# A second block with plain fc1 products, interleaved with block 0's fc2, and weight sums from a second load

## What is computed

```python
h = gelu(einsum('bnd,hd->bnh', x, fc1_w) + fc1_b)            # HID = 1024
shared = einsum('bnh,sh->bns', h, fc2_w) + fc2_b             # 192 outputs
expert = einsum('bnh,bph->bnp', h, experts_w[indices]) + experts_b[indices][:, None]  # 64 outputs
out = x + concatenate([shared, expert], axis=-1)
```

## Time and profile before

| | us |
|---|---|
| median of 3 runs | 380.73 |
| lowest and highest | 380.22, 380.85 |
| the profiled execution, its own time | 380.61 |
| its span in the profile | 378.8 |
| PE busy | 361.0 (95%) |
| ACT, POOL, DVE busy | 248.5, 232.8, 211.8 |

### The profile page before, as it was taken

One profiled execution on the slowest core, in us unless ns is written; L12 is line 12 of the kernel. 1 busy time (PEld: TensorE's weight loads), 2 busy tenths in 40 slices (PEclk: granted clock), 3 DMA queues, 4 the chain that ended last, 5 costly groups with the idle time before them and its releaser, 6 DMA issues.

```text
span 378.8 us, 7987 instructions
## 1 busy us (share of the span) xinstructions
PE 361.0 (95%) x2915; PEld 355.7 (94%) x2915; DVE 211.8 (56%) x357; ACT 248.5 (66%) x420; POOL 232.8 (61%) x105
## 2 busy tenths in 40 slices
PE   6952999999999999999999999999999999999996
PEld 5842999999999999999999999999999999999996
DVE  1477447567473747667373756757384756733331
ACT  2674357687675767777575768767576777755560
POOL 0780537766666777666667776666667766666490
PEclk9995799999999999999999999999999999999999
DMA  8769860616152250616244151626235032303011
GB/s 197 166 140 257 251 135 32 163 40 173 57 146 85 82 130 26 173 54 157 76 110 122 44 154 35 173 58 158 73 91 127 24 115 50 119 2 111 2 56 57
DMA packets 70433, 39.98 MB, mean 106 GB/s; under 512 B 39418, under 2 KB 70394, under 8 KB 70394
## 3 DMA queue, kind: packets, MB, share of 16 engines
q1 hardware_dynamic: 69776, 38.95, 39.0%
q10 hardware_dynamic: 618, 0.53, 0.7%
HBM read 27.92 MB, written 8.39 MB: 96 GB/s over the span
## 4 chain that ended last, share of the span: by engine, by line
PE 86%; issue 2%; POOL 1%; ACT 0%; DVE 0%; POOLq 0%
PE fc_ps L875 39%; PE acc_ps L911 16%; PE acc_ps L915 16%; PE acc_ps L913 16%; POOL ht L303 1%; ACT ht L460 0%; ACT gelu L483 0%; DVE work L710 0%; DVE resid L728 0%; POOLq L293 0%
## 5 line engine op out<-in xcount | busy, mean ns | idle before, releaser
L303 POOL TENSOR_TENSOR ht<-gelu,ht 128x1024 fp32r<-128x1024 f32 x64 | 154.8, 2419 | 115.2 <-ACT ht L460 115.2
L875 PE MATMUL fc_ps<-xt,w1t 128*128 128x256 f32 x1260 | 186.7, 284 | 3.8 <-DVE xt L678 3.8
L875 PEld LDWEIGHTS fc_ps<-xt,w1t 128*128 128x128 f32 x1260 | 167.5, 193 | 4.2 <-DVE xt L678 4.2
L911 PE MATMUL acc_ps<-w2t,ht 128*128 128x256 f32 x512 | 145.5, 284 | 0.1
L913 PE MATMUL acc_ps<-w2t,ht 128*128 128x256 f32 x512 | 145.4, 284 | 0.0
L915 PE MATMUL acc_ps<-w2t,ht 128*128 128x256 f32 x512 | 145.4, 284 | 0.0
L911 PEld LDWEIGHTS acc_ps<-w2t,ht 128*128 128x128 f32 x512 | 98.9, 193 | 0.3 <-POOL ht L303 0.3
L915 PEld LDWEIGHTS acc_ps<-w2t,ht 128*128 128x128 f32 x512 | 98.8, 193 | 0.0
L913 PEld LDWEIGHTS acc_ps<-w2t,ht 128*128 128x128 f32 x512 | 98.8, 193 | 0.0
L446 ACT ACTIVATE work<-fc_ps 128x512 f32<-128x512 f32 x30 | 17.9, 597 | 87.7 <-PE fc_ps L875 87.7
L460 ACT ACTIVATE ht<-gelu 128x1024 fp32r<-128x1024 f32 x64 | 67.8, 1059 | 3.5
(11 more groups left out here) (49 smaller groups left out, 236.5 us busy)
## 6 DMA issues: line engine op xcount, KB each, us to landing
resid<-in_x SPq DMA_DIRECT2D x16, 512.0 KB, 4.0
pieces<-in_L_cond_experts_w SPq DMA_DIRECT2D x128, 64.0 KB, 2.0
out<-resid SPq DMA_DIRECT2D x32, 256.0 KB, 3.2
pieces<-in_x SPq DMA_DIRECT2D x60, 128.0 KB, 3.6
w2t<-w2t SPq DMA_DIRECT2D x4, 768.0 KB, 8.0
bias<-in_L_cond_experts_b SPq DMA_DIRECT2D x32, 32.0 KB, 2.8
pieces<-in_L_cond_fc_w SPq DMA_DIRECT2D x4, 192.0 KB, 7.8
work<-in_L_cond_fc_w ACTq DMA_DIRECT2D x4, 128.0 KB, 5.8
```

What stands on the lines that cost most here:

```text
L303: nc.gpsimd.tensor_tensor(ht[:, slot, LO, :, :].rearrange("p k t -> p (k t)"), gelu[:, q % 2, :, :].rearrange("p k t -> p (k t)"), ht[:, s ...
L875: last = nc.tensor.matmul(fc1_ps[:, dst, j * SEQ:(j + 1) * SEQ], w1t[:, w, wv, ms], xt[:, n % 2, o, xv, :], start=(fresh and j == 0 and at ...
L911: nc.tensor.matmul(dst, h_hi_t, w_hi, start=(r == 0 and u % (2 * T) == 0), stop=True, skip_group_check=True)
```

## The change

Block 1 is now multiplied plainly too (`PLAIN = 2`), so the seven-product loop covers blocks 2 to 15, with all its counts of semaphores moved by one block.

- **PE.** The transposes of the weight sums (`s_bank`) are gone. After block 0's eight chunks come eight pairs of steps: four units of block 0's fc2, then one chunk of block 1's fc1. The chunks of block 1 are taken in the order of pairs 1, 3, 0, 2. fc2 of block 0 no longer waits for the weight sums, and waits for the second copy of fc2_w (`w2_row`) only at its fifth unit.
- **Weight sums.** After the fourth fc1_w transpose group SP loads fc1_w again over its first copy, in 32-row pieces (four DMAs of 256 KB, 256-byte rows). POOL waits for it, makes the four sums, and DVE transposes them (`s_square`) in the transpose bank; ACT and DVE split them as before, in the order 0, 2, 1, 3.
- **POOL.** The sums stand after pair_lo(0) and pair_lo(1) and before pair_lo(2) and pair_lo(3). The low parts of block 1's four pairs are made on DVE instead (`plain_low`).
- **x of block 1** is split whole by ACT and DVE (`x1_high`, `x1_low`).
- **DVE, ACT.** The first work is reordered: two fc2_w transposes ahead of the second half of fc1_w, the fc2_w transposes now in the accumulator banks; experts of block 1, the last `plain_low` and the first drain end DVE's prologue, ahead of the loop.
- **ACT's queue** loads the index first instead of last.

The core of the diff; the shifts of semaphore counts are left out.

```diff
+    PLAIN = 2
...
+    PAIR_ORDER = (1, 3, 0, 2)
...
+        def wait_h_lo(engine, q):
+            if q < PAIRS:
+                engine.wait_ge(h_lo, q + 1)
+            elif q < 2 * PAIRS:
+                engine.wait_ge(plain_lo, q - PAIRS + 1)
+            else:
+                engine.wait_ge(h_lo, q - PAIRS + 1)
+        def chunk_of(q, j):
+            r = q % PAIRS
+            return 2 * (PAIR_ORDER[r] if q // PAIRS == 1 else r) + j
...
+            def load_w1_pieces():
+                for q in range(Q):
+                    sp.dma_start(w1_piece[S * q:S * (q + 1), :, :, :]
+                                 .rearrange("p q k j -> p (q k) j"), w1_pieces[q])\
+                        .then_inc(w1p_loaded, 16)
...
+            sp.wait_ge(w1_tr, 2 * D)
+            load_w1_pieces()
             load_x(1)
...
-            for half in range(2):
-                pool.wait_ge(w1_loaded[half], 16 * Q)
+            pair_lo(0)
+            pair_lo(1)
+            pool.wait_ge(w1p_loaded, 16 * Q)
             weight_sum(0, weight_rows(1, 0), weight_rows(1, 1), ALU.add)
             weight_sum(2, weight_rows(0, 0), weight_rows(1, 0), ALU.subtract)
             pool.wait_ge(s_added, 1)
             weight_sum(1, made(0), weight_rows(0, 0), ALU.subtract)
             pool.wait_ge(s_added, 3)
             weight_sum(3, weight_rows(0, 1), made(1), ALU.subtract)
-            for r in range(PAIRS):
-                pair_lo(r)
-            x_sums_lo(1)
+            pair_lo(2)
+            pair_lo(3)
             pool.wait_ge(b2_loaded, 16)
             pool.wait_ge(x0_tr, D)
             residual(0)
-            for n in range(1, BLOCKS):
+            x_sums_lo(PLAIN)
+            residual(1)
...
+            def x1_high(d):
+                act.wait_ge(x_sq, d + 1)
+                nc.scalar.activation(xt_plain[1][:, d, HI, :], tr_ps[:, d, :], ACT.Copy)\
+                    .then_inc(x1_hi, 1)
...
+            act.dma_start(index_sb[:, :], index.rearrange("(o n) -> o n", o=1))\
+                .then_inc(index_loaded, 16)
             load_w1(act, 0)
             act.dma_start(b1_in[:, :].rearrange("k (q c) -> k q c", q=Q),
                           fc1_b.rearrange("(q k c) -> k q c", q=Q, c=S))\
                 .then_inc(b1_loaded, 16)
-            act.dma_start(index_sb[:, :], index.rearrange("(o n) -> o n", o=1))\
-                .then_inc(index_loaded, 16)
...
             w1_high(1, 0)
             conv_chunk(1)
             w1_high(1, 1)
+            w2_high(0)
+            conv_chunk(2)
             conv_high(0)
-            conv_chunk(2)
-            w2_high(0)
+            w2_high(1)
             conv_chunk(3)
+            w2_high(2)
+            conv_chunk(4)
             conv_high(1)
-            w2_high(1)
-            conv_chunk(4)
-            w2_high(2)
+            w2_high(3)
             conv_chunk(5)
+            for half in range(2):
+                experts_high(0, half)
+            conv_chunk(6)
             conv_high(2)
-            w2_high(3)
-            conv_chunk(6)
+            for d in range(D):
+                x1_high(d)
             conv_chunk(7)
             conv_high(3)
+            conv_chunk(8)
+            conv_chunk(9)
+            conv_high(4)
+            s_high(0)
+            s_high(2)
+            conv_chunk(10)
+            conv_chunk(11)
+            conv_high(5)
+            s_high(1)
+            s_high(3)
+            conv_chunk(12)
+            conv_chunk(13)
+            conv_high(6)
+            b_copy(PLAIN)
+            x_high(PLAIN)
+            conv_chunk(14)
+            x_sums_high(PLAIN)
             for half in range(2):
-                experts_high(0, half)
-            x_high(1)
-            s_high(0)
-            s_high(1)
-            s_high(2)
-            s_high(3)
-            b_copy(1)
-            x_sums_high(1)
-            for n in range(1, BLOCKS):
+                experts_high(1, half)
+            conv_chunk(15)
+            conv_high(7)
...
+            def s_square(s):
+                dve.wait_ge(s_added, S_ORDER.index(s) + 1)
+                nc.vector.transpose(
+                    tr_ps[:, S_ORDER.index(s) % 2, :].rearrange("p (i q c) -> p i q c", i=HALF, c=S),
+                    s_in[:, s].rearrange("p q i c -> p i q c")).then_inc(s_sq, 1)
...
+            def plain_low(q):
+                dve.wait_ge(h_hi, q + 1)
+                nc.vector.tensor_tensor(
+                    ht[:, q % PAIRS, LO, :, :].rearrange("p k t -> p (k t)"),
+                    gelu[:, q % 2, :, :].rearrange("p k t -> p (k t)"),
+                    ht[:, q % PAIRS, HI, :, :].rearrange("p k t -> p (k t)").bitcast(FP32),
+                    ALU.subtract).then_inc(plain_lo, 1)
+            def x1_low(d):
+                dve.wait_ge(x1_hi, d + 1)
+                nc.vector.tensor_tensor(xt_plain[1][:, d, LO, :], tr_ps[:, d, :],
+                                        xt_plain[1][:, d, HI, :].bitcast(FP32), ALU.subtract)\
+                    .then_inc(x1_lo, 1)
...
-            for d in range(D):
-                w1_low(1, d)
             w2_square(0)
             w2_square(1)
+            w1_low(1, 0)
             w2_low(0)
             w2_square(2)
+            w1_low(1, 1)
             w2_low(1)
             w2_square(3)
             w2_low(2)
             w2_low(3)
-            dve.wait_ge(w2_lo, 4)
+            dve.wait_ge(w1_lo, 2 * D)
             for half in range(2):
                 experts_square(0, half)
-            for cols in (slice(0, SHARED), slice(OUT, OUT + SHARED)):
-                nc.vector.tensor_copy(w2t[:, 0, 1, :, cols], w2t[:, 0, 0, :, cols].bitcast(FP32))\
-                    .then_inc(w2_row, 1)
             for half in range(2):
                 experts_low(0, half)
             dve.wait_ge(e_lo, 2)
             for d in range(D):
                 x_square(1, d)
-            for s in range(4):
-                s_low(s)
-            x_sums_first(1)
-            x_low(1, 0)
-            x_sums_last(1)
-            x_low(1, 1)
-            for n in range(1, BLOCKS):
+            for d in range(D):
+                x1_low(d)
+            dve.wait_ge(w2_lo, 4)
+            for cols in (slice(0, SHARED), slice(OUT, OUT + SHARED)):
+                nc.vector.tensor_copy(w2t[:, 0, 1, :, cols], w2t[:, 0, 0, :, cols].bitcast(FP32))\
+                    .then_inc(w2_row, 1)
+            dve.wait_ge(x1_lo, D)
+            s_square(0)
+            s_square(2)
+            plain_low(4)
+            s_low(0)
+            s_low(2)
+            dve.wait_ge(s_lo, 2)
+            s_square(1)
+            s_square(3)
+            plain_low(5)
+            s_low(1)
+            s_low(3)
+            dve.wait_ge(s_lo, 4)
+            for d in range(D):
+                x_square(PLAIN, d)
+            plain_low(6)
+            x_sums_first(PLAIN)
+            x_low(PLAIN, 0)
+            x_sums_last(PLAIN)
+            x_low(PLAIN, 1)
+            dve.wait_ge(xb_lo, 2)
+            dve.wait_ge(t_added, 4)
+            for half in range(2):
+                experts_square(1, half)
+            for half in range(2):
+                experts_low(1, half)
+            plain_low(7)
+            drain(0, 0)
...
                     if u == 0:
-                        pe.wait_ge(h_lo, q + 1)
+                        wait_h_lo(pe, q)
                         if r == 0:
                             pe.wait_ge(e_lo, 2 * (n + 1))
                             if n == 1:
                                 pe.wait_ge(w2_copied, 16 * 2 * R)
-                    if r == 0 and u == 0 and n == 0:
-                        pe.wait_ge(s_lo, 4)
-                        pe.wait_ge(w2_row, 2)
+                    if r == 0 and n == 0:
+                        if u == 0:
+                            pe.wait_ge(w2_lo, 4)
+                        elif u == 2 * T:
+                            pe.wait_ge(w2_row, 2)
...
             conv_chunk(4)
-            s_bank(0)
             conv_chunk(5)
-            s_bank(1)
             conv_chunk(6)
             conv_chunk(7)
-            s_bank(2)
-            s_bank(3)
-            for n in range(1, BLOCKS):
+            for at, (r, first) in enumerate(((0, 0), (1, 0), (0, 4), (1, 4),
+                                             (2, 0), (2, 4), (3, 0), (3, 4))):
+                fc2_units(0, r, first, 4)
+                if at == 0:
+                    pe.wait_ge(x1_lo, D)
+                conv_chunk(K + at)
+            for n in range(PLAIN, BLOCKS):
```

More of the change, by code:

```diff
@@ L55, in cond_mlp_residual @@
     w1_v = fc1_w.rearrange("(q k c) d -> q c k d", q=Q, c=S)
+    w1_pieces = fc1_w.rearrange("(m r) (q j) -> q r m j", r=S, q=Q)
     w2_v = fc2_w.rearrange("(a r) (q j) -> q r a j", r=S, q=Q)
@@ L103, in cond_mlp_residual @@
         tr_ps = psum("tr_ps", [P, 2, BANK])
-        xt0 = xt[:, 0, 0:4, :, :].rearrange("p (d v) h t -> p d v (h t)", d=D)
+        xt_plain = [xt[:, n, 0:4, :, :].rearrange("p (d v) h t -> p d v (h t)", d=D)
```

(27 more changed lines are left out.)

132 lines of the change are left out of this document (70 added, 62 removed).

## The result

The change makes the kernel a little slower: 381.35 us (median of 20 runs, 380.13 to 382.84) against 380.29 us for the kernel before (20 runs, 379.59 to 381.11), a ratio of 1.003 with a 95% interval of 1.0018 to 1.0041. The forecast was 379.0. The profiled execution is one of the quicker ones: 380.52 us, with a span of 378.7 us. The profiled execution of the kernel before, 380.61 us, lies 0.3 above its median.

What follows compares the result with a forecast made beforehand. Bound: PE's own work from 42 us on, and a preparation chain between 24 and 37 us. 61.8 - 57.9 = 3.9 us gained, less 2.3 for the clock, leaves 1.6 off 380.61: 379.0 us; range 375.3 to 382.8.

Steps and rivals of the forecast that it cites:

- PE's own part: Block 0's fc2 and block 1's plain fc1 ahead of the loop, run back to back and done at 50.1 us.
- the sums: GpSimd's four weight sums of 1.29 us each, starting when the fc1_w pieces land at 29.7 and ending at 35.1 us.
- the mechanism named: On SP's queue, loads issued behind the fc2_b broadcast wait for it, so the fc1_w pieces land at 29.7 us.
- plain_low(7) is held by residual(1): On the shared port, GpSimd's back-to-back work holds plain_low(7) 1.6 us, so it reads near 2.9 us.
- The mark: Start of the loop's first fc2 matmul (line 911 before); it must come before 61.8 us for a gain.
- a tie: On VectorE, plain_low(4) is ready within 0.3 us of residual(0)'s start; assumed to go first, the other outcome costing 2.0 us.
- the forecast mark of 57.9: Loop's first fc2 matmul at 57.9 us: 56.2 by the preparation chain alone, plus plain_low(7) held 1.6 us.
- the 3.9 us counted as gained at the mark: At the loop's first fc2 matmul: 61.8 - 57.9 = 3.9 us gained, before the low clock's 2.3 us.
- rival (b): plain_low(4) loses to residual(0) on the shared port: +2.0 us, 381.0 us, no measurable difference; chance 0.17.
- The w2_row casts, which I had costed at nothing: Copies for w2_row end near 31 us, before block 0's fc2 needs them at its fifth unit, 32.8 us; no cost.
- "The same 2.3 us": PE idle from 50.1 us to the loop's first fc2 matmul makes the clock fall again, costing 2.3 us as before.
- 50.8: Ceiling: the loop's first fc2 matmul if nothing but PE's own work were late, 11 us better.

Runs made afterwards that it cites:

- e5: Changed kernel with the four fc1_w pieces issued ahead of the expert biases and the fc2_b broadcast; 377.91 us, ratio 0.9951 against the kernel before.
- e10: Changed kernel with throwaway matmuls in all four holes of PE; 379.23 us, ratio 0.9975 against the kernel before.
- e2: Changed kernel with GpSimd's residual(0) made to wait for plain_low(4); 379.52 us, ratio 0.9985 against the kernel before.
- e6: Changed kernel with 24 throwaway matmuls before and 44 behind the first product; 379.45 us, ratio 0.9984 against the kernel before.
- e7: Changed kernel with pieces ahead of the broadcast, residual(0) after plain_low(4), residual(1) after plain_low(7), drain(0,0) ahead of plain_low(7); 373.69 us, ratio 0.9822.
- e4: Changed kernel with drain(0,0) ahead of plain_low(7) on VectorE; 376.92 us, ratio 0.9912 against the kernel before.
- e1: Changed kernel with GpSimd's residual(1) made only after the last plain_low; 379.66 us, ratio 0.9985 against the kernel before.
- e9: The four edits of e7 on the changed kernel, plus 14, 7 and 16 throwaway matmuls in PE's holes; 372.01 us, ratio 0.9784.
- again: The changed kernel unchanged, run for a second profile; 381.37 us, ratio 1.0028 against the kernel before.

## Why the prediction was wrong, point by point

**What held.** PE's own part came out as worked: chunk 4 at 18.35 (18.3 forecast), block 0's fc2 at 25.89 (25.8), block 1's first chunk at 28.55 (28.5), PE done near 49.9 (50.1), no hole between. The pieces start the sums at 29.40 (29.7), by the mechanism named: moved ahead of the broadcast they are there in time. High of pair 4 ends at 40.1 (39.9). plain_low alone takes 1.20 to 1.25 us (1.22). plain_low(7) is held by residual(1), 2.64 us in all (2.9). The mark waits for the drain. The Trainium skill's rule on the shared port ("SBUF — State Buffer", Who interferes with whom), that the one which comes second waits for the whole first operation, now has this kernel's numbers: 3.32 us against 1.23, nearly the whole of residual(0). The hold is what is left of GpSimd's operation, less 0.14 us: 2.10 us of 2.24 left for plain_low(4), 1.42 of 1.56 for plain_low(7). The 0.3 us of the kernel before, which I read as a sign that the hold is short, fits that too: GpSimd had only 0.46 us left there.

**The step that failed: "plain_low(4) is ready within 0.3 us of the start of residual(0), a tie; I let it go first".** The tie was lost in all seven profiles that keep that order, by 0.14 to 0.17 us, also where the pieces land early (e5) or 1.3 us late (e10). So it is no toss-up: both sides start from the end of pair_lo(2), one through pair_lo(3), the other through two GELUs and a high copy, and in every one of these profiles the first is the shorter. It costs 2.1 us (e2), takes the forecast mark of 57.9 to 60.0, and with it most of the 3.9 us counted as gained at the mark. I had put this down as rival (b), with a chance of 0.17 and 381.0 us; its mark and its 2.0 us are what happened. My own chain spoke for it: pair_lo(3) would end at 37.4 + 2.4 = 39.8 us and the high copy at 39.9. Giving the nearer outcome the smaller chance was the error.

**From the mark to the median.** The forecast was 1.6 us under the profiled execution of the kernel before. The profiled execution of the changed kernel is 0.1 under it: the mark is 2.3 us later than forecast (2.1 by the tie and 0.7 by the sums, less 0.3 by the earlier landing and 0.2 of small terms), and the low clock took 0.8 less (both below). The medians stand at +1.1 instead, since the kernel before has its median 0.3 us below its profiled execution and the changed kernel 0.8 above.

**A term that was mis-sized: the sums.** Counted from 29.7 to 35.1, they took 5.88 us, 0.7 more than the four of 1.29. The w2_row casts, which I had costed at nothing because their reader on PE waits later, are running on VectorE when the first sum starts. In e10, where the sums start after the casts, they take 5.18. The earlier they start beside the casts, the longer both take: 6.20 us and 2.67 for the casts in e2, 6.58 and 3.76 in e6.

**The clock.** A fall came, but at 53.2 us and for 10.2 us, not near 56 for some 5. "The same 2.3 us" was too much for what lies behind the mark: the 18 matmuls from it to the 24th take 3.66 us instead of 2.16, so 1.5 in the first profile (1.8 in the second). The other 0.7 of the kernel before was its first product, and here that runs while PE waits anyway. By medians the low clock costs the kernel before 2.65 us (380.08 against 377.43) and the changed one 2.1 (381.37 against 379.23), so this term is not what turned the sign. It also varies: the stretch ends earlier or later (63.4 and 64.2 us), and there can be others, near 27 us after a hole of 1.8 us (the second profile, e6, e7) and near 11 us (e6, e7). With PE kept busy the runs close up, which makes these falls the likely reason why the medians of 381.35 and 381.37 stand 0.8 us above the first profiled execution. That is not shown for any single run without a profile, and a late landing of the pieces, 0.7 us at the mark in e10, adds to the spread.

**Where the expected gain went.** The preparation gives the mark at 60.2 instead of 50.8: the pieces wait behind the broadcast (3.6 us at the mark, e5), plain_low(4) behind residual(0) (2.1, e2), the drain behind plain_low(7) and that behind residual(1) (3.6 together, 1.4 of them the port's; e4, e1). The gains are not wholly separate: they sum to 9.3 us, and together they bring the mark to 53.13, 7.1 us earlier.

**What stays open.** Why the clock falls near 27 us in some executions and not in others of the same kernel was not settled; the hole in front of it is the same to 0.1 us. The fall near 11 us came in the two profiles in which PE had stood idle longest ahead of the first transposes of fc1_w, 2.05 us until 9.3; in the eleven others it was 0.4 to 1.8. No run changed that hole, so this is not shown to be the cause. Why the fall near 53 us comes earlier or later is open too.

## What to carry to other kernels

When work is moved from GpSimd to VectorE, look for each GpSimd operation that runs when the moved one becomes ready: a VectorE operation with two SBUF inputs then pays the rest of it, and being 0.2 us behind costs over 2 us here. Where a forecast comes out as a tie, follow both sides back to their common start and give the side that is ready first, by however little, the larger chance. An accumulator's drain belongs ahead of any operation whose result is needed later, and a load that a chain waits for ahead of a slow broadcast on the same queue. Holes that PE has in the prologue are worth filling with throwaway matmuls on both sides before a change is judged: here that alone gave the kernel before 2.65 us, more than twice the 1.1 us by which the change moved the medians.

## What was not expected of the hardware

- Issuing took longer behind a slow transfer: the four issues of the second load take SP 9.49 us behind the broadcast (one of them 6.86), and 3.22 to 4.89 us in the three profiles in which they go ahead of it (e7, e5, e9).

```profile
L270 SPq DMA_DIRECT2D work<-in_L_cond_fc_w x4: 504/998/6860, 15.5 to 23.8; - x4
```

- The granted clock can fall after a hole of 1.8 us that follows a busy stretch, in some executions of a kernel only: it did in "again" and not in the first profile of the same kernel.
- A cast on VectorE that is under way when GpSimd starts a sum lengthens it: 5.88 us for the four sums against 5.18. The casts grow as well: from 1.82 us for the two to 2.67 in e2.
